# Edge rows of a graph network on one NeuronCore: the last chunk of 81 batches goes back from single-row fetches to GpSimd's gather

## What is computed

```
def gat_conv(x, edge_index, W, att_src, att_dst, bias):     # twice
    h = (x @ W).reshape(N, HEADS, HEAD_DIM)
    e = a_src[src] + a_dst[dst]                 # one logit per edge and head
    e = jnp.where(e > 0, e, NEG_SLOPE * e)
    ex = jnp.exp(e - segment_max(e, dst)[dst])
    alpha = ex / (segment_sum(ex, dst)[dst] + 1e-16)
    return segment_sum(h[src] * alpha[:, :, None], dst) + bias
# then, with z the normalized sum of x and the two layers:
msgs = z[edge_dst] @ Wd + z[edge_src] @ Ws + edge_weight[:, None] * ww + bm
agg = segment_max(msgs, edge_dst)
hidden = relu(z @ W1a + agg @ W1b + b1); out = layernorm(z + hidden @ W2 + b2)
```

## Time and profile before

| | us |
|---|---|
| median of 3 runs | 9003.74 |
| lowest and highest | 8996.88, 9019.71 |
| profiled execution | 9009.38 |
| its span (first to last instruction) | 9007.6 |

### The profile page before, as it was taken

How to read it: one execution, slowest core, us unless ns; L and a number is a source line. 1 busy time by engine, 2 the same in 40 slices (tenths; PEclk the granted TensorE clock), 3 DMA queues, 4 the chain that set the end, 5 groups by cost and what they waited for, 6 DMA issues and landing times.

```text
span 9007.6 us, 143351 instructions
## 1 busy us (share of the span) xinstructions
PE 5521.4 (61%) x24591; PEld 4999.4 (56%) x24591; DVE 4968.3 (55%) x13366; ACT 2072.5 (23%) x3605; POOL 5058.2 (56%) x5130
## 2 busy tenths in 40 slices
PE   4666666666666566666666666663555555555556
PEld 4666666666665466665666666652444444444445
DVE  2655555555555535555555555574665656566667
ACT  2322222222222432222222222251000000000005
POOL 4456555555655645555555555546565555555562
PEclk5555555555555655555555555565767666667679
DMA  5222222222222322222222222244445554454554
GB/s 148 61 67 68 64 65 67 67 66 66 66 71 51 87 66 63 66 69 65 65 68 64 69 66 66 69 116 121 130 128 130 128 132 120 129 127 128 132 138 137
DMA packets 737828, 812.61 MB, mean 90 GB/s; under 512 B 180058, under 2 KB 552228, under 8 KB 736772
## 3 DMA queue, kind: packets, MB, share of 16 engines
q1 hardware_dynamic: 565448, 469.89, 18.9%
q0 software_dynamic: 157376, 329.33, 15.8%
q10 hardware_dynamic: 14076, 3.80, 0.2%
HBM read 753.63 MB, written 48.89 MB: 89 GB/s over the span
## 4 chain that ended last, share of the span: by engine, by line
ACTq 28%; issue 25%; SPq 12%; ACT 11%; PE 9%; DVE 7%; another core or an unknown queue 5%; DMA 1%; DVEq 1%; POOL 1%; POOLq 0%
ACTq L1271 18%; ACTq L1253 7%; ACT st L1326 5%; ACT st L1321 4%; SPq L498 4%; PE bA L982 3%; PE bS L1038 3%; DVE acc L1669 3%; SPq L478 2%; ACTq L1269 2%; SPq L722 2%; SPq L720 2%; DVE S L1677 1%; PE bE L1038 1%
## 5 line engine op out<-in xcount | busy, mean ns | idle before, releaser
L868 POOL DMA_INDIRECT G<-table,idx x3268 | 3234.8, 990 | 2426.8 <-issue 966.0
L1038 PE MATMUL bS<-G,S 128*128 x8816 | 2179.6, 413 | 1022.8 <-issue 338.2
L1038 PEld LDWEIGHTS bS<-G,S 128*128 128x128 f32 x8816 | 1880.3, 300 | 1155.1 <-issue 826.2
L982 PEld LDWEIGHTS bA<-adst,st 128*128 128x128 f32 x7872 | 1769.5, 330 | 1354.7 <-ACT st L1326 883.7
L982 PE MATMUL bA<-adst,st 128*128 x7872 | 1775.6, 350 | 1164.5 <-ACT st L1326 781.4
L868 POOL DMA_INDIRECT G<-ztable,idx x1634 | 1594.9, 976 | 1125.1 <-issue 441.8
L1669 DVE TENSOR_TENSOR acc<-acc,bS 128x136 f32 (+1 forms) x4408 | 1277.7, 290 | 769.9 <-remote 394.3
L1321 ACT ACTIVATE st<-xd,neg_p 128x512 f32<-128x512 bf16 x972 | 700.9, 721 | 3984.7 <-issue 2770.3
L1677 DVE TENSOR_TENSOR S<-iota_row,nd 128x512 f32<-128x512 f32 x1404 | 962.2, 686 | 0.3
L1665 DVE SCALAR_TENSOR_TENSOR acc<-bS,acc 128x132 f32 x610 | 179.4, 294 | 1076.4 <-remote 407.8
L889 PE MATMUL bA<-ident,G 128*128 128x128 f32 x1637 | 349.8, 359 | 609.1 <-DVE ch L1942 318.2
(11 more groups left out here) (224 smaller groups left out, 3831.7 us busy)
## 6 DMA issues: line engine op xcount, KB each, us to landing
xd<-d_drel SPq DMA_DIRECT2D x328, 384.0 KB
xd<-in_ew SPq DMA_DIRECT2D x312, 256.0 KB
st<-d_neg SPq DMA_DIRECT2D x312, 256.0 KB
wide<-table ACTq DMA_DIRECT2D x4608, 0.5 KB
G<-table,idx POOLq DMA_INDIRECT x3268
wide<-table SPq DMA_DIRECT2D x2304, 0.5 KB
wide<-ztable ACTq DMA_DIRECT2D x2304, 0.5 KB
isend<-in_ew SPq DMA_DIRECT2D x104, 256.0 KB
```

What stands on the lines that cost most here:

```text
L868: pool.indirect_dma_start(G[:, r, c, 0:width], None, from_table, bass.IndirectOffsetOnAxis(ap=idx[:, r, c:c + 1], axis=0)).then_inc(gather ...
L982: mm = pe.matmul(bA[:, bass.ds(chunks[s], HEADS)], st[:, i % 3, s, :], adf[:, bass.ds(tiles[s], HEADS)], start=False, stop=True, skip_grou ...
L1038: mm = pe.matmul(bank_of(l, u, r, k)[:, j * w:(j + 1) * w], S[:, onehots(r, i), s, :], chunk_at[0][s], start=True, stop=True)
```

## The change

All chunks of all batches are gathered by GpSimd; ACT and SP send no rows, load no lists of them and wait for nothing on their account. DVE's copy of the chunk and the waits for it on DVE and PE go. GpSimd's gathers rise from 4902 to 4983. The tiles `wide` and `regs_wide` and the input of lists go. Who makes which one-hots stays as it was: ACT those of `expand_quad`, DVE those of `select_pair` in the layers and the maximum. The core of the diff (the definitions of `registers`, `wide_rows` and `wide_part` are taken out on both engines):

```diff
-WIDE_C = CB - 1
-WIDE_R = (3, 4, 2)
-WIDE_BY = (ENG.SP, ENG.Activation, ENG.Activation)
-WIDE_EVEN = ((4, 0, 32), (3, 32, 64), (2, 64, 96), (1, 96, P))
-WIDE_EARLY = ((3, 0, 55), (2, 55, 110), (1, 110, P))
-WIDE_LATE = ((4, 0, 37), (3, 37, 92), (2, 92, P))
-WIDE_N = 9
...
         def rows_landed(l, b, r, it):
             short = 16 * (CB - LAST_C)
             ends = (l if r == LAST_B % RING else 0) + (1 if chunks_of(b) < CB else 0)
-            if r in WIDE_R and not isinstance(it, int):
-                return 496 * landed(0, r, it) + 16 + l * (512 * B_OF[r] - 16 * WIDE_N) - short * l * (r == LAST_B % RING)
-            return 512 * landed(l, r, it) - short * ends - 16 * wide_sofar(l, r, it)
+            return 512 * landed(l, r, it) - short * ends
...
 # SP, a layer's batch
-                    wide_part(l, b, r, it, 0, 4)
                     if not isinstance(b, int) or b + RING < UNITS:
                         exp_load(l, b + RING, r, it + 1)
                     sel_load(l, b + 2, (r + 2) % RING, it + (r + 2) // RING)
-                    wide_part(l, b, r, it, 1, 4)
...
 # SP, the maximum
                         step_load(b, st_)
-                        wide_part(l, b, r, it, st_, NS)
...
 # GpSimd
-                    for c in range(WIDE_C if wide_at(l, b, r, it) else chunks_of(b)):
+                    for c in range(chunks_of(b)):
...
 # PE, the maximum
-                    if s == NS - 1 and wide_at(l, b, r, it):
-                        pe.wait_ge(*wide_landed(l, r, it))
-                        pe.nop(nofuse=True)
                     for j in range(SC):
-                        from_wide = s * SC + j == WIDE_C and wide_at(l, b, r, it)
-                        frm = wide[:, WIDE_R.index(r), 0:HID] if from_wide else G[:, r, s * SC + j, 0:HID]
-                        tr = turn(Y_bank[s % 2][:, j * P:(j + 1) * P], frm)
+                        tr = turn(Y_bank[s % 2][:, j * P:(j + 1) * P], G[:, r, s * SC + j, 0:HID])
...
 # ACT, a layer's batch
                         if i == 4:
                             weights(b, r)
-                        wide_part(l, r, it, i, UQ)
...
 # ACT, the maximum
-                        wide_part(l, r, it, s, NS)
...
 # DVE, a layer's batch
-                    if wide_at(l, b, r, it):
-                        dve.wait_ge(*wide_landed(l, r, it))
-                        dve.nop(nofuse=True)
-                        vec.tensor_copy(G[:, r, WIDE_C, 0:TW], wide[:, WIDE_R.index(r), :]).then_inc(wide_used, 1)
-                        dve.wait_ge(wide_used, wide_copied(l, r, it))
-                        dve.nop(nofuse=True)
                     dve.wait_ge(gathered[r], rows_landed(l, b, r, it))
```

More of the change, by code:

```diff
@@ L9 @@
 BF16 = mybir.dt.bfloat16
-U16 = mybir.dt.uint16
 ALU = mybir.AluOpType
@@ L73 @@
 EPS = 1.0e-5
-assert all(0 < r < RING and RING * WIDE_N + r < LAST_B for r in WIDE_R)
 assert KB * P == NCH and KB <= KQ and HEADS * CB == P and NH * 2 == NT
@@ L124, in columns, with gnn_program @@
     return slice(at, at + widths[name])
-def gnn_program(nc, x, xt, dst_rows, dst_ends, dst_last, d_idx, d_wide, d_ew, first, rest, out):
+def gnn_program(nc, x, xt, dst_rows, dst_ends, dst_last, d_idx, d_ew, first, rest, out):
     with ExitStack() as ctx:
@@ L325, in x_groups @@
             return 16 * (NG // XR + (1 if k < NG % XR else 0))
[L327 to L375, removed]
         def rows_landed(l, b, r, it):
@@ L1250, in scalar_program @@
             act.dma_start(c_first[:, :], first).then_inc(in_first, 16)
-            def registers(v):
-                _, values = nc.values_load_multi_w_load_instructions(
-                    v, engines=[ENG.Activation], min_val=0, max_val=N_NODES - 1, bass_reorder=False,
-                    skip_runtime_bounds_check_because="the source of an edge is a node")
-                return values
-            def wide_rows(l, k, it, lo, hi):
-                to, width = (table[l], TW) if l < 2 else (ztable, HID)
-                sem_in, _ = wide_landed(l, WIDE_R[k], it)
-                if lo == 0:
-                    act.wait_ge(*wide_listed(l, k, it))
-                    act.nop(nofuse=True)
-                    if wide_free(l, WIDE_R[k], it) is not None:
-                        act.wait_ge(*wide_free(l, WIDE_R[k], it))
-                        act.nop(nofuse=True)
-                rows = [to[bass.ds(at, 1), :] for at in registers(regs_wide[0:1, k, lo:hi])]
-                for row in rows:
-                    act.lower_ap_dma(row)
-                for j, row in enumerate(rows):
-                    act.dma_start(wide[lo + j:lo + j + 1, k, 0:width], row).then_inc(sem_in, 16)
-            def wide_part(l, r, it, j, parts):
-                for k in range(NW):
-                    if WIDE_BY[k] != ENG.Activation:
-                        continue
-                    for at, lo, hi in wide_steps(k, r, it):
-                        first, last = lo + (hi - lo) * j // parts, lo + (hi - lo) * (j + 1) // parts
-                        if last > first:
-                            wide_rows(l, k, at, first, last)
-                    at = wide_list_due(k, r, it)
-                    if j == parts - 1 and at is not None:
-                        act.dma_start(regs_wide[0:1, k, :], d_wide[bass.ds(RING * at + WIDE_R[k], 1), :]).then_inc(wide_idx_act, 16)
             def attention(l, frm):
@@ L2079, in layouts @@
         "idx": padded(src, E_PAD, 0).reshape(NB, CB, P).transpose(0, 2, 1),
-        "wide": padded(src, E_PAD, 0).reshape(NCH, P)[CB - 1::CB].astype(np.uint16),
         "ew": padded(edge_weight, E_PAD, 0),
```

46 lines of the change are left out of this document (2 added, 44 removed).

## The result

| | before | after |
|---|---|---|
| median of the runs, us | 9006.65 | 8652.17 |
| lowest and highest after | | 8646.28, 8657.68 |
| ratio, 95% interval | | 0.9603 (0.9588 to 0.9618) |
| span of the profiled execution | 9007.6 | 8654.0 |

What follows compares the result with a forecast made beforehand. ACT's issue of rows was taken to bound the layers' batches, SP's rows and loads the maximum's. Gains of 180 (layer 0), 185 (layer 1) and 203 us (maximum) sum to 568; 9009 - 568 = 8441, said as 8440, range 8180 to 8800.

Steps and rivals of the forecast that it cites:

- all slots alike: Layer loops: with the rows gone, batches of every slot should last alike, about 49 us.
- lead of the last gather of batch 20: Layer 0: this gather ended 23 us before DVE took its rows; shorter batches would take at most some 8 us.
- The middle between 47.1 and 51.5: Layer loops: a batch without rows was put at 49.3 us, gaining 180 us in layer 0 and 185 in layer 1.
- rival 2: Loops: gathers and PE lock in part, layer and maximum batches end at 51.5 us; gain 212 us, 8797; chance 0.20.
- The added gathers at nothing: GpSimd: 81 more gathers were priced at nothing, being covered by their lead; fully in the open, 101 us.
- ACT's issue as the length of a batch: Layer loops: nine quads of about 5.8 us on ACT make 52.5 us, the length of a batch.
- The third sign: Fewer rows, shorter batch: slot 0 with 36 ACT rows takes 50.4 us, slot 3 with 55 takes 55.9.
- Rival 1: Loops: the number of gathers sets the time, 81 x 1.69 = 137 us slower, 9146; chance 0.11.

Runs made afterwards that it cites:

- e3: Kernel after the change, gathering only 24 of 32 chunks from the sixth batch on (1119 gathers fewer): 8027 us, 0.8908 of the kernel before.
- e1: Kernel before with ACT's rows undone, so only SP sends rows: 8893 us, 0.9873 of the kernel before.
- e2: Kernel before with SP's rows undone, so only ACT sends rows: 8865 us, 0.9837 of the kernel before.
- e5: Kernel after the change, GpSimd waiting every 8th chunk instead of every second: 6942 us on a quick chip, 0.9723 of the kernel before.
- e8: Kernel after the change with all batches written out, no loops: 6907 us on a quick chip, 0.9676 of the kernel before.
- e6: Kernel after the change, gathers released a batch earlier: 6933 us on a quick chip, 0.9715 of the kernel before.

## Why the prediction was right in sign and range, and wrong in size

| step of the prediction | forecast | measured |
|---|---|---|
| rows leave ACT's and SP's chain | yes | ACTq 0%, SPq 0% |
| all slots alike | yes | 49.9 to 54.3 in layer 0 |
| layer 0, us a batch; gain | 49.3; 180 | 51.6; 76 |
| layer 1 | 49.3; 185 | 50.5; 131 |
| maximum | 48.0; 203 | 49.2; 148 |
| 81 added gathers | 0 | about 45, an estimate |
| outside the loops | 0 | -2 |
| lead of the last gather of batch 20 | at least 15 | 21 |
| GpSimd's busy share | near 60% | 59% |

*The middle between 47.1 and 51.5.* This is the step that failed. I had two samples without rows: batches 1 and 2, and batch 49. Batch 49 was the one paced like the loop, I said so, and then took the middle because its two values lay 9 us apart. The loop came out at batch 49's level (51.6 and 50.5), and batch 49 itself takes 55.60 and 54.77 now, without a row anywhere. That the mean of its two values, 51.5, hit the loop so closely is partly luck. The upper end was the estimate to take; it is rival 2, 8797, and the result lies a little nearer to it (145 us) than to my forecast (212). The same holds for the maximum with 49.2, between my 48.0 and rival 2's 51.5.

*The added gathers at nothing.* The reason given was the lead of 23 us, and the lead did stay (21 us). It is no cover: e3 shows that gathers cost although their data are early. That they do so through the signals they hold up is how I read the traces; no run shows it by itself. By e3's 0.56 us the 81 gathers cost 81 x 0.56 = 45 of the 212 us missed. This is an estimate, since e3 takes away eight gathers from a batch where the change adds one.

*ACT's issue as the length of a batch.* The arithmetic (nine quads of 5.8 us are 52.5) carried one quad over to all. In the trace of before all that is recorded of ACT and its sequencer, between the first `distance` of a batch and that of the next, adds up to 41 to 46 us with 55 rows and 33 with 36 (layer 0), less than the 50 to 56 us of the batches. e1 and e2 show that the rows of one issuer alone are worth 0.5 to 1.7 us a batch wherever they stand, in the chain or not. The third sign, "fewer rows, shorter batch", was a pair picked from five: slot 0 is short (50.1) and slot 1 long (54.3) without a row too, and slots 1, 2 and 4 with the same 55 rows as slot 3 were there to compare.

*Rival 1* is refuted as a fixed price (1.61 us per gather after, 1.94 in e3), but what it started from, PE held up beside GpSimd's gathers, is what the traces of the kernel after show on the slow chips (20.2% of layer 1's chain in releases of unknown origin). The other 170 us or so of the miss lie in the difference between batches 1 and 2 (47 us) and the loop (51), with the same 32 gathers each. e5 and e8 were to tell pacing and loop registers apart and met a quick chip, where neither removes the like difference (35 and 40 us) and the store of gathers makes it. On the slow chip the store doesn't run out (lead 17 us or more in every batch of layer 0), so that reason does not hold there. It stays open.

The rule of the Trainium skill ("Perfetto Trace Analysis", DMA Optimizations) that I weighed, to spread DMAs over engines when descriptor generation is the bottleneck, fits GpSimd on the quick chips, whose gathers follow each other without a pause there. Even there the measurement decides against the rows: the kernel with fewer gathers and rows on ACT and SP takes 7146 us, the one without rows 6939.

## What to carry to other kernels

A chain that lies for a third on one sequencer tells what was last, not how much later it was than the next path. Compare all batches with much and little of the suspected work, not one pair. Look for a stretch in which that engine already does nothing, take the one whose waits are like the loop's, and don't average it with a kinder one. If a share of the chain ends in an unknown queue while another engine sends indirect DMAs without a pause, price these DMAs by a run with fewer of them before calling them hidden, and look at the same kernel on a second chip.

## What the runs showed of the hardware

- Chips differ by a fifth of the time on this program: 9005 and 9139 us on two, 7146 us on two others for the kernel before; 8652 and 6939 for the kernel after. Durations of single instructions agree (by the median a gather takes 944 and 945 ns, L873 354 and 354 ns).
- At a layer's start on the slow chip the late signals come one by one at a fixed distance (`ex_done` at 100.22, 122.61 and 145.01 us in layer 0), 22.4 us apart, while the gathers come every 1.25 us. The chain shows the same in layer 1:

```profile
3032.70 20.84 another core or an unknown queue
3055.10 20.84 another core or an unknown queue
3077.50 20.84 another core or an unknown queue
```

- One indirect gather of 128 rows holds GpSimd for 0.94 + 0.30 us by the median on both kinds of chip, beside working engines and alone; 32 of them to a batch are the floor of 40 us that the quick chips reach.
- Writing out the loops of five batches (52 batches on every engine) gained 32 us of 6939; these two runs met two different chips (before: 7146.4 and 7145.7 us), but against e5 and e6 on its own chip it is 35 and 26 us.
